# Source rows of the output written from the merged state in each step, and two pairs a step

## The reference

```python
qkv = x @ W
q, k, v = jnp.split(qkv, [Fqk, 2 * Fqk], axis=-1)
...
aw = jnp.einsum('ehf,ehf->eh', q[src], k[dest])
m = jax.ops.segment_max(aw, src, num_segments=n)
e = jnp.exp(aw - m[src])
denom = jax.ops.segment_sum(e, src, num_segments=n)
alpha = e / denom[src]
out = jax.ops.segment_sum(alpha[:, :, None] * v[dest], src, num_segments=n)
...
x = _layernorm(x + out)
```

## Time and profile before

| what | us |
|---|---|
| median of 3 runs | 2148.97 (2148.57 to 2158.34) |
| the profiled execution | 2156.94 |
| its span, first to last instruction | 2155.2 |
| TensorE busy | 1803.9 (84%) |
| VectorE busy | 1434.7 (67%) |
| ScalarE busy | 1149.2 (53%) |
| GpSimd busy | 949.1 (44%) |

### The profile page before, as it was taken

The page is one execution under the profiler, slowest core; times in us unless marked ns, Lnnn a source line. Parts: engine busy times, 40 slices in busy tenths (PEclk is TensorE's granted clock), DMA queues, the critical chain, the costliest instruction groups (busy, mean ns, idle before and its releaser), DMA issues. The chain is left out here.

```text
span 2155.2 us, 24520 instructions
## 1 busy us (share of the span) xinstructions
PE 1803.9 (84%) x5525; PEld 933.2 (43%) x5525; DVE 1434.7 (67%) x2621; ACT 1149.2 (53%) x2356; POOL 949.1 (44%) x1070
## 2 busy tenths in 40 slices
PE   5999999599999999999999995961881588998840
PEld 2444444244444444444444443531771344544420
DVE  5365554177777777777777773517995578787876
ACT  1344434255555555555555552224883878877853
POOL 2212102166666666656666663544553232333236
PEclk8999999799999999999999997985555689999965
DMA  7752102534444454444444445554556887878774
GB/s 250 250 206 63 27 13 31 142 134 172 171 159 166 157 172 172 165 164 155 169 172 172 163 153 188 105 87 156 110 119 178 257 242 221 238 212 241 200 212 144
DMA packets 167421, 350.61 MB, mean 163 GB/s; under 512 B 30481, under 2 KB 30962, under 8 KB 166838
## 3 DMA queue, kind: packets, MB, share of 16 engines
q1 hardware_dynamic: 130838, 247.28, 32.4%
q0 software_dynamic: 33168, 98.01, 20.4%
q10 hardware_dynamic: 3344, 4.51, 0.7%
HBM read 177.32 MB, written 153.71 MB: 154 GB/s over the span
## 5 line engine op out<-in xcount | busy, mean ns | idle before, releaser
L687 PE MATMUL d_p_h<-w3a,d_xT 128*128 128x512 f32 x632 | 285.6, 595 | 23.2 <-DMA d_xT<-in_xT 23.2
L687 PE MATMUL d_p_p<-d_wr,d_x1T 128*128 128x512 f32 x632 | 288.3, 600 | 0.0
L687 PE MATMUL d_p_o<-d_w,d_uT 128*128 128x512 f32 x632 | 284.5, 593 | 3.0 <-ACT d_uT L762 3.0
L562 POOL TENSOR_SCALAR d_small<-d_mv 128x1 f32<-128x1 f32 x158 | 77.6, 491 | 296.7 <-DVE d_mv L813 148.7
L851 DVE TENSOR_TENSOR d_zz<-d_yg,d_xbeta 128x512 f32<-128x512 f32 x79 | 136.9, 1733 | 96.3 <-POOL d_yg L902 96.3
L687 PEld LDWEIGHTS d_p_h<-w3a,d_xT 128*128 128x128 f32 x632 | 120.7, 191 | 175.6 <-issue 175.6
L687 PEld LDWEIGHTS d_p_o<-d_w,d_uT 128*128 128x128 f32 x632 | 119.8, 190 | 153.7 <-issue 149.1
L755 ACT ACTIVATE d_yn<-d_y,d_small 128x512 f32<-128x512 f32 x79 | 64.3, 814 | 228.2 <-POOL d_small L567 228.2
L687 PEld LDWEIGHTS d_p_p<-d_wr,d_x1T 128*128 128x128 f32 x632 | 115.6, 193 | 116.5 <-issue 116.5
L783 ACT ACTIVATE d_x<-d_zz,d_small 128x512 f32<-128x512 f32 x79 | 64.2, 813 | 174.9 <-POOL d_small L567 174.9
L294 PE MATMUL m_p_H<-m_xT,m_w 128*128 128x512 f32 x320 | 146.8, 613 | 4.8 <-ACT m_xT L335 4.8
(11 more groups left out here) (286 smaller groups left out, 4080.9 us busy)
## 6 DMA issues: line engine op xcount, KB each, us to landing
sum_counted<-m_tile_sum SPq DMA_DIRECT2D x10, 2112.0 KB
state<-d_empty SPq DMA_DIRECT2D x80, 264.0 KB, 2.4
update<-d_empty SPq DMA_DIRECT2D x80, 256.0 KB, 2.3
pair_x<-x SPq DMA_DIRECT2D x40, 512.0 KB
out_rows<-pair_rows SPq DMA_DIRECT2D x40, 512.0 KB
d_xT<-in_xT SPq DMA_DIRECT2D x79, 256.0 KB
d_z<-sum_counted SPq DMA_DIRECT2D x79, 256.0 KB
d_x<-in_x SPq DMA_DIRECT2D x79, 256.0 KB
```

Source lines behind the costliest of these rows:

```text
L562: nc.gpsimd.tensor_scalar(tmp, var, factor, add, ALU.mult, ALU.add).then_inc(done, 1)
L687: last = nc.tensor.matmul(out[:, :], lhsT[:, c, :], w[:, c, :], start=(c == 0), stop=(c == KB - 1))
```

## The change

The source rows are made in the loop. Right after `merge` the state of tile e lies in the buffer `new`. `attend(e)` on VectorE divides it by its denominators, adds the x3 rows in place in `src_rows_sb` and takes the statistics; `source_rows(e)` on ScalarE normalises in place; both run once in each of the steps 4 to 23. The second gathers of the sums and the loops over G behind the main loop are gone. The state of a node is complete only in the last tile that has it, so `seen` now counts equal sources in later tiles. GpSimd scatters the rows in the last three steps (`scatter_out`): tiles 0 to 7, 8 to 16 and 17 to 19, after it has waited for all pair stores.

The pairs are spread anew: 2 in each of the steps 0 to 19 and none in the last four, where it was 3, 3, 2, 2 and then 2 and 1 in turn, with 1 and 2 at the end. ScalarE may take 4 tiles a step, where it was 3. Four pairs are loaded plainly, where it was three, and the early fill of the fourth is gone.

```diff
@@ -53,7 +53,7 @@
 PLAIN_BUFS = 0
 PAIRS = NODE_TILES // 2
 ROW_BUFS = 4
-PLAIN = 3
+PLAIN = 4
@@ -1100,9 +1100,10 @@
 
             dve.wait_ge(src_in, 16)
-            ready(nc.vector.memset(seen[:, 0:1], 0.0))
-            for t in range(1, T):
-                ready(nc.vector.tensor_scalar(equal[:, 0:t * P], rows_i[:, 0:t * P], col_f[:, 0, t:t + 1], None,
+            ready(nc.vector.memset(seen[:, T - 1:T], 0.0))
+            for t in range(T - 1):
+                later = min((t + 1) * P, LAST_START)
+                ready(nc.vector.tensor_scalar(equal[:, later:E], rows_i[:, later:E], col_f[:, 0, t:t + 1], None,
                                               ALU.is_equal, ALU.add, accum_out=seen[:, t:t + 1]))
             ready(nc.vector.tensor_scalar(seen[:, :], seen[:, :], float(ROWS), None, ALU.mult))
             ready(nc.vector.tensor_tensor(out_f[:, :], seen[:, :], one_f[:, 0, :], ALU.add))
@@ -1181,7 +1182,8 @@
 def plain_plan(steps):
-    plan = [3, 3, 2, 2] + [2 - i % 2 for i in range(steps - 6)] + [1, 2]
+    plan = [2] * (steps - 4) + [0] * 4
     assert sum(plan) == PAIRS
     return plan
@@ -1191,7 +1193,7 @@
     given, done, tiles = 0, 0, []
     for step in range(len(plan) + 1):
-        n = given - done if step < 5 or step == len(plan) else min(given - done, 3)
+        n = given - done if step < 5 or step == len(plan) else min(given - done, 4)
...
@@ -1340,7 +1339,6 @@
                 pair_load_p(nc, k, sp, j)
             for j in range(2):
                 pair_load_x1(nc, k, sp, j)
-            pair_fill(nc, k, sp, PLAIN)
             sp.wait_ge(scattered, 16 * T)
...
@@ -1676,6 +1668,12 @@
                 pool.wait_ge(merged, t + 1)
                 pool.indirect_dma_start(k.state[:, :], at_rows(k.unique[:, 0, t:t + 1]), new[:, :], None
                                         ).then_inc(gone, 16)
+            def scatter_out(t):
+                pool.wait_ge(out_done, t + 1)
+                pool.indirect_dma_start(k.out[:, :], at_rows(k.unique[:, 1, t:t + 1]), k.src_rows_sb[:, t, :], None,
+                                        bounds_check=N - 1, oob_is_err=False).then_inc(out_gone, 16)
...
                 if step + 2 < T:
                     gather_rows(step + 2)
                 if step + 1 < STEPS:
-                    for j in range(given, given + HERE[step + 1]):
+                    for j in range(max(given, PLAIN), given + HERE[step + 1]):
                         pair_add_p(nc, k, pool, j)
                     given += HERE[step + 1]
-            pool.wait_ge(gone, 16 * T)
-
-            def gather_sums(g):
-                if g >= SUM_BUFS:
-                    pool.wait_ge(att, 2 * (g - SUM_BUFS + 1))
-                for s in range(2):
-                    pool.indirect_dma_start(sums[g % SUM_BUFS][:, s, :], None, k.state[:, :],
-                                            at_rows(k.index[:, 0, 2 * g + s:2 * g + s + 1])
-                                            ).then_inc(sums_in[g % SUM_BUFS], 16)
-
-            def scatter_rows(g):
...
+            def source_rows(t):
+                b, row = t % 2, k.src_rows_sb[:, t, :]
+                act.wait_ge(o_ready, t + 1)
+                reciprocal_deviation(nc, k, act, o_mv[b][:, 1:2], o_neg[b], o_rstd[b][:, :], o_shift[b], o_sc, 3 * t)
+                nc.scalar.activation(row, row, ACT.Identity, bias=o_shift[b][:, 0:1], scale=o_rstd[b][:, 0:1]
+                                     ).then_inc(out_done, 1)
...
+                if 0 <= e < T:
+                    source_rows(e)
                 for u in range(unit + early + between, unit + TILES[step]):
                     tile_normalise(nc, k, act, u)
                 unit += TILES[step]
-            for g in range(G):
...
+            def attend(t):
+                b, row, mean = t % 2, k.src_rows_sb[:, t, :], part[:, :, 0:HD]
+                dve.wait_ge(merged, t + 1)
+                if t:
+                    dve.wait_ge(att, t)
+                nc.vector.reciprocal(inv[:, :], state_parts(new)[:, :, HD]).then_inc(inv_done, 1)
+                dve.wait_ge(inv_done, t + 1)
+                if t:
+                    dve.wait_ge(o_y_done, t)
+                nc.vector.tensor_tensor(mean, state_parts(new)[:, :, 0:HD],
+                                        inv[:, :].rearrange("p (h a) -> p h a", a=1).to_broadcast([P, HEADS, HD]),
+                                        ALU.mult).then_inc(att, 1)
+                dve.wait_ge(att, t + 1)
+                nc.vector.tensor_tensor(row.rearrange("p (h f) -> p h f", h=HEADS), mean,
+                                        row.rearrange("p (h f) -> p h f", h=HEADS), ALU.add).then_inc(o_y_done, 1)
+                dve.wait_ge(o_y_done, t + 1)
+                if t >= 2:
+                    dve.wait_ge(out_done, t - 1)
+                nc.vector.bn_stats(o_stats[b][:, :], row).then_inc(st, 1)
+                dve.wait_ge(st, t + 1)
+                nc.vector.bn_aggr(o_mv[b][:, :], o_stats[b][:, :]).then_inc(mv_done, 1)
+                dve.wait_ge(mv_done, t + 1)
+                nc.vector.tensor_scalar(o_neg[b][:, :], o_mv[b][:, 0:1], -1.0, None, ALU.mult).then_inc(o_ready, 1)
...
                 if a < T:
                     softplus(a)
+                if 0 <= e < T:
+                    attend(e)
                 for j in range(pair + 1, pair + HERE[step]):
                     pair_leaky(nc, k, dve, j)
                     pair_means(nc, k, dve, j)
```

More of the change, by code:

```diff
@@ L1219, in pair_fill @@
     b = j % ROW_BUFS
-    if j >= ROW_BUFS:
-        sp.wait_ge(k.pair_gone[b], 16 * (j // ROW_BUFS))
-    else:
-        sp.wait_ge(k.quotient_done, 1)
+    sp.wait_ge(k.pair_gone[b], 16 * (j // ROW_BUFS))
     sp.dma_start(k.pair_rows[b][:, :, :], k.quotient[:, :].rearrange("p (a d) -> p a d", a=1).to_broadcast([P, 2, D])
@@ L1621, in values_phase @@
                              "part", "merged", "gone"))
[L1624 to L1633 removed]
+        inv = sb("inv", [P, HEADS])
+        o_stats, o_mv = ([sb(f"o_{n}{i}", [P, w]) for i in range(2)] for n, w in (("stats", 6), ("mv", 2)))
+        o_neg, o_rstd, o_shift = ([sb(f"o_{n}{i}", [P, 1]) for i in range(2)] for n in ("neg", "rstd", "shift"))
+        inv_done, att, o_y_done, st, mv_done, o_ready, o_sc, out_done, out_gone = (
+            sem(n) for n in ("inv", "att", "o_y", "st", "mv", "o_ready", "o_sc", "out", "out_gone"))
+        WRITTEN = (0, 8, T - 3, T)
         HERE = plain_plan(STEPS)
@@ L1656, in _ @@
             pair_store(nc, k, sp, PAIRS - 1)
-            for b in range(ROWS_AHEAD):
-                sp.wait_ge(out_gone[b], 32 * len(range(b, G, ROWS_AHEAD)))
+            sp.wait_ge(out_gone, 16 * T)
         @block.gpsimd
@@ L1949, in _ @@
                 unit += TILES[step]
-            for g in range(G):
-                b, rows = g % 2, y[g % ROWS_AHEAD]
-                act.wait_ge(o_ready, g + 1)
-                reciprocal_deviation(nc, k, act, o_mv[b][:, :, 1], o_neg[b], o_rstd[b][:, :], o_shift[b], o_sc, 4 * g)
-                for s in range(2):
-                    nc.scalar.activation(rows[:, s, :], rows[:, s, :], ACT.Identity, bias=o_shift[b][:, s:s + 1],
-                                         scale=o_rstd[b][:, s:s + 1]).then_inc(out_done, 1)
         @block.vector
```

59 lines of the change are left out of this document (6 added, 53 removed).

## The result

The changed kernel takes **2163.14 us** (median of 19 runs, 2152.03 to 2169.76) against 2154.18 for the kernel before, run beside it (19 runs, 2148.57 to 2162.53): ratio 1.0032 (95% interval 1.002 to 1.0044). The forecast was 7 us less; it came out 9 us more. Both lie within the 0.5% around no change, and 2163 lies in the range, but the sign is wrong. The profiled execution has a span of 2163.5 us against 2155.2.

A forecast was written before the change was run, and what follows sets the result against it. The prediction took a loop of waits, with no engine full, to bound the kernel. Start -17, loop +66 (step 18.7 to 22.8 us), step after +4, end -60 summed to -7 us: 2142 us, range 2120 to 2168.

The forecast's parts named there:

- Start, -17: Start of the last stage: needed pairs arrive earlier, so the first merge comes about 17 us sooner, at 1712.6.
- ScalarE's chain, 22.0: Main loop: one step's work and waits followed on ScalarE, with four tiles and the source rows, take 22.0 us.
- the 0.8: Main loop: 0.8 us a step added for two equally long loops with varying DMA times, also holding unhidden clock loss.
- the clock rival: Main loop: TensorE's clock drops each step, slowing queries and values; step 24.3 us, total 2166 us; chance 17%.
- My sign for it: Main loop, trace after: merges above 24 us apart would make the 0.8 us allowance wrong.
- the rival of late buffers: Main loop: pair buffers come free too late; step 24.2 us at worst, 23.4 if half the time, total 2152; 12%.
- GpSimd's loop, 22.1: Main loop: pair store, fill, adds, state scatter and gather over GpSimd take 44.2 us for two steps, 22.1 a step.
- The step after, +4: Step from merge 17 to 18: no pair but still four tiles, about 21 us against 16.95, a loss of 4.
- The end, -60: After merge 18: second gathers of the sums go, GpSimd's queue remains; 49.7 us instead of 109.8, a gain of 60.
- The rule: TensorE in the loop: long idling starts each burst at low clock; forecast took part as hidden, the rest within 0.8 us.

The follow-up runs named there:

- e_warm2: Changed kernel plus spare products (matmuls no one reads) on TensorE: seven ahead of the queries, four ahead of the scores' spread; 2151.3 us, ratio 0.9983 to the kernel before.
- e_bufs: Changed kernel with five pair buffers instead of four; 2162.1 us, ratio 1.0 to the kernel before.
- e_warm2_bufs: Changed kernel with the spare products of e_warm2 and five pair buffers; 2146.1 us, ratio 0.9965 to the kernel before.
- e_pairs: Kernel before with only the new spread of pairs (two a step, four tiles a step, four plain pairs), source rows still behind the loop; 2185.4 us, ratio 1.0132.
- e_early: Changed kernel with seven spare products ahead of the queries and ScalarE's tiles dealt one early, two middle, one late instead of 2, 1, 1; 2146.3 us, ratio 0.9946.
- e_rows_warm: Changed kernel with the old spread of pairs and all row scatters at the end, plus the spare products of e_warm2; 2192.4 us, ratio 1.018 to the kernel before.
- e_warm: Changed kernel plus ten spare products ahead of the queries only, in steps 4 to 19; 2165.4 us, ratio 1.0035 to the kernel before.
- e_early_bufs: e_early with five pair buffers instead of four; 2123.3 us, ratio 0.9864 to the kernel before.

## Why the prediction was wrong

- **Start, -17: right**, -15.1. The first merge is at 1714.5 against 1712.6.
- **ScalarE's chain, 22.0: right as a chain, and it was all there.** In the step shown ScalarE waits 0.67 for slow queries, which I had at 0, and 2.21 for `attend`, which I had at 1.1; VectorE had lost 1.19 to slow values. 22.0 + 0.67 + 1.19 = 23.9, the 23.87 of that step (the 1.19 is what makes the wait for `attend` longer by 1.1).
- **The step that failed is the 0.8.** "By the rows a part is hidden and the rest sits in my 0.8" is where the clock rival's 24.3 was weighed and put at 17%. Its mechanism is what happened: slow queries exceed the second tile (0.67 of the 1.1 given), slow values meet a waiting VectorE (1.19 in each step, where I had 1.2 on average). I had read the earlier trace rows right but taken "full speed after most" of the waits as evidence for the step to come. Those steps had shorter waits, 1.8 us on average, as this line of the kernel before over 1760 to 2040 us says:

```profile
PE f_p_qv L1762 <- ACT same_dst L1842: 21.9, 12, 2.2
```

  The new one has 3.7 on average, in every step. I had even worked out that TensorE would idle about 5 us there, and gave it no weight.

  The 0.8 stood for two loops of equal length that disturb each other. No such thing shows: the merges come every 23.8 to 24.1 us, and in the loop VectorE never waits for a pair add. It was taken from the 1.4 us of excess in the kernel before, and part of that was slow queries already, 1.2 us a step where the step that I followed had 0.49:

```profile
ACT same_dst L1888 <- PE f_p_qv L1762: 14.2, 12, 3.2
```

  So the cost that failed is that of TensorE's slow matmuls, priced inside 0.8 us a step; they cost 1.9 to 2.0 (23.87 against 21.85 in the one step without them). My sign for it, merges above 24 us apart, stood too high to catch this.
- **What the clock is worth.** The spare products alone give 0.85 us a step (e_warm2), 1.1 with the buffers out of the way (e_bufs to e_warm2_bufs). With that, the step is 22.7 and the time 2146, near the forecast of 22.8 and 2142. That is in part luck: e_warm2_bufs has a fifth buffer, its values still run slow in many steps, and nothing in it answers to the 0.8. The full price in the changed kernel, about 2 us a step, is read from its own rows; the spare products give back 1.1 of it.
- **The clock rival's 2166: near 2163 in part by luck.** It stood for 17 us more than the 2148.97 known then. Measured are 9 more: its step was 24.3 and not 23.8, and the end gained 5 us more than it had. (The range calls the same rival 2168, which is a slip, and in the rival of late buffers a step of 24.2 in half of the cases gives 23.2 with the loop's 22.1, not 23.4; nothing hangs on either.)
- **GpSimd's loop, 22.1: not the bound here.** Its pieces were off both ways: store to fill 2.65 us (1973.09 to 1975.74) not 3.8, fill to second add 3.64 not 4.9, the adds landing after 6.4 us (5.6 to 7.2) not 8.1, but from the state's scatter to the gather 7.5 (1980.58 to 1988.11; 6.2 at 1909.80) not 5.8:

```profile
1979.38 0.90 POOL L1230 DMA_DIRECT2D pair_rows<-p_rows  x1 [11.35 <-DMA pair_rows<-pair_quotient]
1980.58 1.05 POOL L1669 DMA_INDIRECT state<-f_new,unique  x1 [0.30 <-issue]
1988.11 1.05 POOL L1664 DMA_INDIRECT f_old<-state,index  x1 [6.48 <-DMA state<-f_new,unique]
```

  It shows as soon as slow matmuls and source rows don't hide it: VectorE waits for pair adds in e_pairs, e_warm2 and e_early, and in the last two a fifth buffer gives 0.24 and 1.1 us a step.
- **The step after, +4: short by 2.** 22.85 against 21: it has the same four tiles, and the queries (6.71, at 2093.23) and values (5.37, at 2102.75) are as slow as in the steps ahead of it.
- **The end, -60: right in kind, -64.7.** The row scatters run at 1.30 us as counted. The state's landing was the mis-sized term: when no pairs move, the next gather comes 3.0 us after the scatter, not 5.8, twice (at 2119.41 and here):

```profile
2136.20 0.97 POOL L1669 DMA_INDIRECT state<-f_new,unique  x1 [1.60 <-DVE f_new L2027]
2139.19 0.98 POOL L1664 DMA_INDIRECT f_old<-state,index  x1 [2.03 <-DMA state<-f_new,unique]
2140.48 1.01 POOL L1675 DMA_INDIRECT out_rows<-src_rows_sb,unique  x1 [0.30 <-issue]
...
2156.69 0.98 POOL L1675 DMA_INDIRECT out_rows<-src_rows_sb,unique  x1 [0.30 <-issue]
```

- **The rule.** The rows show idle time of 3.6 us ahead of each burst and queries of 6.6 to 6.7 us behind it, in every step of the loop but one (5.40, at 1736.88). The Trainium skill, TensorE: Matmul & The Clock Gate, section HAM oscillation, describes this for a loop that waits for DMAs, bursts that start at the low clock after each long wait; the trace agrees, here behind waits for ScalarE. I had cited it and let a few rows of a kernel with shorter waits outvote it.

The sum of the chain is shown for the changed kernel, by its step without slow values (21.85) and by the others (23.87), and e_rows_warm shows that the loop with source rows shortens by 2.4 us a step once the clock is held; that the spare products act through the clock alone is inferred from their having no reader and from the rows of queries and values that they changed.

## What to carry over

When work is added to a loop in which TensorE is not the bound, work out how long TensorE will idle in one piece, and price the matmuls behind that wait at half clock unless something hides them; check whether what they delay lies on the loop that sets the step. Spare products are a cheap probe for it, but they must cover each of the long gaps, or the slow spell moves to the next one (e_warm). And undo a limit before judging the one beneath: the fifth buffer was worth nothing in the changed kernel and 1.1 us a step once the order of the tiles and the clock were mended (e_early to e_early_bufs).

## What the runs showed that I had not expected

- Two parts of the change cost 2.9 and 4.9 us a step alone and 5.1 together. Alone, the pairs have VectorE wait for pair adds and the rows have ScalarE wait for slow queries; together, the first of these waits is gone. That the longer of two limits sets the step, and not their sum, fits this, but no run proves it.
- Behind idle time of only 2.07 us the spread took 3.65 us instead of 2.05, and the values 5.38 instead of 3.70 (e_warm; in every other step only the values were slow).
- A trapped loop is very regular: the merges of the changed kernel come every 23.8 to 24.1 us from 1761 us on, while those of e_early_bufs vary from 20.0 to 23.3.
